# Chunk loop of a decoder layer: in each paired half the state products are issued first and the output products behind them, instead of in turn

## The chip, the cores and the metric

The kernel runs on one core of one Trainium2 chip. The metric is the device time of one execution in microseconds. The median of the runs before the change is 1487.71 us.

## The reference

One decoder layer on x of shape (4, 1024, 256): x plus a gated delta-rule attention of layernorm(x), plus a differential cross attention on a context of 64 tokens, plus a mixture-of-experts feed-forward. The change lies in the first part, a recurrence over the tokens with 16 heads of 16 x 16 state:

```python
def step(Sst, inp):
    qt, kt, vt, bt, gt = inp
    Sd = gt[..., None, None] * Sst
    kS = jnp.einsum('bhk,bhkv->bhv', kt, Sd)
    Snew = Sd + jnp.einsum('bhk,bhv->bhkv', kt, bt[..., None] * (vt - kS))
    ot = jnp.einsum('bhk,bhkv->bhv', qt, Snew)
    return (Snew, ot)
```

## The kernel before

The 1024 tokens are cut into 8 blocks of 128 tokens (times 4 batch rows), and each block into 8 chunks of 16 tokens. Within a chunk the recurrence is turned into small matrix products; from chunk to chunk the state is carried. Three stages of neighbouring blocks run side by side on every engine, in an order written out by hand in the tables `ORDERS`: a word such as `cs.3.1` is one call of the stage function `cs_` with chunk 3 and half 1, and the engines are tied by semaphore counters (`up` waits for one, `fin` raises one). TensorE works through its list in this order.

For each chunk c the chain of the recurrence is: `d1` (TensorE, L1943, old state times keys and queries) raises `d1_ps`; DVE's `m` (L1407) builds the operand `rq`; `cs` (TensorE) forms the state products (`state_product`, L1951) and, for the chunk before, the output products (`out_product`, L1957); DVE's `o` (L1425, L1428) sums up the output and waits for `co_ps`; DVE's `s` (L1414) updates the state and waits for `cs_ps`; the next `d1` waits for the state. On DVE, `o` of chunk c-1 stands ahead of `s` of chunk c. `z` (TensorE, L1926) prepares a later chunk; it goes over two row halves `a` in its outermost loop, over two groups g and four batch rows in the inner ones, with 64 x 32 weights and 128 moving columns.

The products of `cs` are fp32 with 32 x 64 weights and 64 moving columns. The state product takes rows 64k + 32*half, the output product the other strip of 32 rows, 64k + 32*(1-half); both take the 64 columns from 64a, and they write to different PSUM banks (k and 2 + k). A chunk is done in two halves; the second waits for the first through `cs_half`. In chunk 0 there is no output product, and the last chunk's output products are issued by `co` alone. Both products are called from `cs_`, L1966 to L1979.

Of the kernel before, what the change touches and what calls it, by code (L numbers as in the profile page):

```python
# [36 lines left out]
G = 2  # L37
# [292 lines left out]
def build(nc, x, out, weights, consts, cols, scratch, biases):  # L330
    ctx = ExitStack()
    with ctx:
# [1347 lines left out]
        def _(pe):  # L1680
# [73 lines left out]
            def first(i):  # L1754
                def up(name, k=1):
                    pe.wait_ge(ev[name].sem, ev[name].at(i, k))

                def fin(name, ins):
                    ins.then_inc(ev[name].sem, 1)
# [187 lines left out]
                def state_product(c, g, k, a, half):  # L1947

                    q, p_ = slice(64 * a, 64 * a + 64), slice(64 * k + 32 * half, 64 * k + 32 * half + 32)
                    dst = bank[k][q, 0:D].rearrange("p (h n v) -> p h n v", h=4, v=DH)[:, :, 2 * g + half, :]  # L1950
                    return mm(dst, zc_ring[p_, c % 4, 2 * a + g, 1, :], rq[p_, c % 2, (2 * a + g) * 64:(2 * a + g) * 64 + 64].rearrange("p (h v) -> p h v", h=4), start=True, stop=True)  # L1951

                def out_product(c, g, k, a, half):

                    q, p_ = slice(64 * a, 64 * a + 64), slice(64 * k + 32 * half, 64 * k + 32 * half + 32)
                    dst = bank[2 + k][q, 0:D].rearrange("p (h n t) -> p h n t", h=4, t=CH)[:, :, 2 * g + half, :]
                    return mm(dst, rq[p_, c % 2, (2 * a + g) * 64:(2 * a + g) * 64 + 64], zc_ring[p_, c % 4, 2 * a + g, 0, :].rearrange("p (h t) -> p h t", h=4), start=True, stop=True)  # L1957

                def cs_(c, half):

                    if half:
                        up("cs_half", c + 1)
                    else:
                        up("r", c + 1)
                        up("zc", min(c + 3, 8) if c else 1)
                        if c > 1:  # L1966
                            up("o", c - 1)
                    for g in range(G):
                        for k in range(2):
                            for a in range(2):  # L1970
                                last = state_product(c, g, k, a, half)
                                if c:
                                    last_out = out_product(c - 1, g, k, a, 1 - half)
                    if half == 0:
                        fin("cs_half", last_out if c else last)
                    else:
                        fin("cs_ps", last)
                        if c:
                            fin("co_ps", last_out)  # L1979
# [19 lines left out]
                def wo_(k):  # L1999
                    if k == 0:  # L2000
# [9 lines left out]

                return {"turn1": turn1, "rot": rot, "unrot": unrot, "cond": cond, "gate": gate, "proj": proj, "db": db, "btr": btr, "brep": brep, "sum": sum_, "vturn": vturn, "decay": decay, "grow": grow,
                        "raw": raw, "z": z, "d1": d1, "cs": cs_, "co": co, "onorm": onorm, "wo": wo_}

            def second(j):
# [258 lines left out]
```

How the kernel before makes its waits and increments, by code:

```python
    def wait(self, step=None):  # L92
        step = self.count if step is None else step
        self.eng.wait_ge(self.sem, self.i * self.per + step if self.per else step)
# [510 lines left out]
        @block.sync  # L606
# [11 lines left out]
            load_weights(["cin"], ld_cin)
            load_scratch(ramp, "ramp", ld_ramp)
            sp.dma_start(bias_row, biases[:, :]).then_inc(ld_b, 16)
            load_weights(["dw", "ctrl"], ld_proj)
            for n, name in enumerate(("wk", "wv", "ctx")):
                load_scratch(stage[:, 512 * n:512 * n + 512], name, ld_ctx)
            load_scratch(stage[:, 2048:3072], "ctxd", ld_ctx)
            load_weights(["wo", "ffu"], ld_rest)
            sp.wait_ge(su["split"], 1)
            for n in range(3):
                sp.dma_start(bias3[n:n + 1, :].rearrange("o (p n) -> o p n", p=NBR), bias_part[n]).then_inc(ld_b3, 16)
# [7 lines left out]
            def store(n):  # L639
                sp.wait_ge(ev["done"].sem, ev["done"].at(n, 2))
                sp.dma_start(rows(out, n).rearrange("b p d -> p b d"), ot[:, :, :]).then_inc(x_out.sem, 16)
# [1 line left out]
            def load_residual(i):  # L644
                sp.wait_ge(ev["tinv"].sem, ev["tinv"].at(i))
                load(xres, xres_in, i)
# [1 line left out]
            def values(i):  # L649
                sp.wait_ge(ev["vt_sb"].sem, ev["vt_sb"].at(i, 2))
                if i:
                    sp.wait_ge(v_in.sem, v_in.at(i - 1, 64))
                    sp.wait_ge(ev["r"].sem, ev["r"].at(i - 1, 8))
# [31 lines left out]
                def fin(name, ins):  # L686
                    ins.then_inc(ev[name].sem, 1)
```

## Time and profile before

| | |
|---|---|
| median of 3 runs | 1487.71 us (1486.2 to 1487.97) |
| profiled execution | 1491.12 us, span of its instructions 1489.1 us |
| PE busy, matmul | 1393.9 us, 94% |
| DVE busy | 1180.6 us, 79% |
| ACT busy | 835.1 us, 56% |
| chain that ended last | PE 76%, DVE 16%, ACT 5% |
| records of L1951 and of L1957 | 2048 each |

PE is TensorE's matmuls, PEld its weight loads, DVE VectorE, ACT ScalarE. The chain is followed back from the last instruction; at each step it goes to what released an instruction, or to the one ahead of it on its engine. A matmul's start in the trace is recorded, its end is modelled.

### The profile page before, as it was taken

To read this page: it belongs to the slowest core of one execution; us is meant where nothing else is said; L and a number is where in the kernel's file an instruction comes from. 1 tells how busy PE (TensorE), PEld (TensorE's weight loads), DVE (VectorE), ACT (ScalarE), POOL (GpSimd) and SP (SyncE) were. 2 spreads that over 40 slices of the span, in tenths; PEclk is the share of its full clock that TensorE was granted. 3 is DMA by queue.
4 is the path that set the end of the run, shared out by engine and by line. 5 is a ranking of instruction groups with operands and counts; after the bars stand their busy time and mean duration, and the time that the engine had idled before them with its cause. 6 is when DMAs were issued, how large, how long until landed. Compare 5 with 4: busy or idle time off the path is not lost.

```text
span 1489.1 us, 38165 instructions
## 1 busy us (share of the span) xinstructions
PE 1393.9 (94%) x15812; PEld 921.4 (62%) x15836; DVE 1180.6 (79%) x3196; ACT 835.1 (56%) x1599; POOL 218.3 (15%) x221
## 2 busy tenths in 40 slices
PE   5988999999999999999999999999999988898999
PEld 2555566656765566655766566655666557756765
DVE  6558888987898878987897878987897868965663
ACT  2455465646665565646666565655666555544453
POOL 1130220102300211102301122002300022000000
PEclk9999999999999999999999999999999999999999
DMA  6011010000100011000110001000100001000000
GB/s 239 0 30 30 2 30 29 3 1 16 30 30 2 2 39 27 10 2 15 30 30 2 1 20 25 31 1 9 36 15 3 2 15 30 17 2 16 1 1 15
DMA packets 20212, 31.27 MB, mean 21 GB/s; under 512 B 1480, under 2 KB 17864, under 8 KB 19784
## 3 DMA queue, kind: packets, MB, share of 16 engines
q1 hardware_dynamic: 20040, 28.82, 6.6%
q8 instruction: 126, 2.06, 0.6%
q14 instruction: 46, 0.38, 0.1%
HBM read 20.41 MB, written 8.39 MB: 19 GB/s over the span
## 4 chain that ended last, share of the span: by engine, by line
PE 76%; DVE 16%; ACT 5%; issue 2%; DMA 0%; POOL 0%; ACTq 0%; SPq 0%; DVEq 0%
PE bank L2139 14%; PE bank L1686 6%; PE bank L1816 6%; PE bank L2077 6%; PE four L1907 4%; PE bank L1711 3%; PE bank L2040 3%; PE bank L2062 3%; PE bank L1736 3%; PE four L1951 3%; PE bank L1819 3%; PE bank L1718 2%; PE four L1711 2%; PE four L1957 2%; PE four L1926 2%
## 5 line engine op out<-in xcount | busy, mean ns | idle before, releaser
L2139 PE MATMUL bank<-w_sb,cs 128*128 128x512 f32 x512 | 245.7, 597 | 1.2 <-ACT qkv L1029 0.3
L736 POOL TENSOR_TENSOR decayed<-state,pk 128x512 f32<-128x512 f32 x64 | 75.2, 1174 | 813.2 <-DVE state L1414 813.2
L1029 ACT ACTIVATE cs<-bank 128x512 f32<-128x512 f32 x112 | 66.7, 596 | 150.8 <-PE bank L1692 77.8
L2139 PEld LDWEIGHTS bank<-w_sb,cs 128*128 128x128 f32 x512 | 94.4, 190 | 90.3 <-issue 84.7
L2077 PEld LDWEIGHTS bank<-vx_sb,cs 128*128 128x128 f32 x896 | 108.9, 189 | 25.9 <-ACT cs L979 13.7
L2077 PE MATMUL bank<-vx_sb,cs 128*128 128x136 f32 x896 | 118.4, 283 | 5.4 <-ACT cs L979 3.7
L1816 PE MATMUL bank<-hT,w_sb 128*128 128x512 f32 (+1 forms) x224 | 110.6, 617 | 2.6 <-ACT rota L832 0.8
L971 ACT ACTIVATE cs<-cs 128x1024 f32<-128x1024 f32 x60 | 63.5, 1058 | 77.6 <-DVE cs L1504 77.5
L979 ACT COPY cs<-bank 128x512 f32<-128x512 f32 x114 | 66.4, 582 | 72.4 <-PE bank L2062 72.1
L1626 DVE SCALAR_TENSOR_TENSOR cs<-cs,rwt 128x256 f32<-128x256 f32 x196 | 85.6, 487 | 19.8 <-ACT cs L1029 19.8
L1273 DVE SCALAR_TENSOR_TENSOR qkv<-pre,l_sb,qkv 128x512 f32<-128x512 f32 x144 | 100.2, 746 | 0.0
L1498 DVE TENSOR_REDUCE pkc<-bank 128x8 f32<-128x512 f32 x116 | 75.1, 684 | 28.6 <-PE bank L2040 28.6
L771 ACT ACT_TABLE_LOAD x66 | 84.7, 1283 | 1.2
L2062 PE MATMUL bank<-c_sb,cs 128*128 128x128 f32 x456 | 73.3, 284 | 11.7 <-DVE cs L1525 8.2
L2040 PE MATMUL bank<-kbx,cs 32*128 32x256 f32 x464 | 77.1, 400 | 1.4 <-ACT cs L966 1.4
L1951 PE MATMUL four<-rq,shared 32*64 32x64 f32 x2048 | 61.9, 230 | 17.1 <-DVE rq L1407 9.4
L1686 PE MATMUL bank<-cs,w_sb 128*128 128x256 f32 (+1 forms) x304 | 75.2, 385 | 1.3 <-DVE cs L1561 0.9
L1951 PEld LDWEIGHTS four<-rq,shared 32*64 32x64 f32 x2048 | 44.1, 131 | 49.6 <-DVE rq L1407 22.0
L1504 DVE TENSOR_TENSOR cs<-bank,pkc 128x512 f32<-128x512 f32 x116 | 74.2, 681 | 0.0
L2062 PEld LDWEIGHTS bank<-c_sb,cs 128*128 128x128 f32 x456 | 49.1, 141 | 40.5 <-issue 27.7
L718 POOL TENSOR_TENSOR shared<-kn,c_sb 128x512 f32<-128x512 f32 x32 | 34.3, 1071 | 256.7 <-DVE kq L1310 219.5
L1414 DVE SCALAR_TENSOR_TENSOR state<-four,c_sb,decayed 128x128 f32<-128x128 f32 x256 | 71.5, 342 | 0.0
(284 smaller groups left out, 3090.7 us busy)
## 6 DMA issues: line engine op xcount, KB each, us to landing
xt<-in_x SPq DMA_DIRECT2D x8, 512.0 KB, 4.8
vscr<-qkv SPq DMA_DIRECT2D x8, 512.0 KB, 2.6
vT<-vscr SPq DMA_DIRECT2D x32, 128.0 KB, 4.4
Tm<-in_x SPq DMA_DIRECT2D x8, 512.0 KB, 3.8
out<-cs SPq DMA_DIRECT2D x8, 512.0 KB, 2.9
w_sb<-in_weights SPq DMA_DIRECT2D x1, 3656.0 KB, 18.8
w_sb<-in_weights SPq DMA_DIRECT2D x1, 1456.0 KB, 8.5
cs<-in_scratch SPq DMA_DIRECT2D x3, 256.0 KB, 8.4
```

Source lines behind the costliest of these rows:

```text
L736: fin("dec", tt(decayed[:, :, :, :], state[:, :, :, :], eGC[:, c, :].unsqueeze(1).unsqueeze(3).to_broadcast([P, 4, G * B, DH]), ALU.mult))
L771: nc.scalar.preload_act_table_set(name)
L1273: ins = stt(dst, pre[:, n % 4, :, t:TB + t], L("conv", 4 * n + t, 4 * n + t + 1), dst, ALU.mult, ALU.add)
L1498: highest[a] = link(red(mx[:, a, :], sc[a], AX.X, ALU.max))
L1626: ins = stt(comb[:, b, :], src, wgt, comb[:, b, :], ALU.mult, ALU.add)
L1686: last = mm(dst, lhs(k), rhs(k), start=k == 0, stop=k == n - 1)
L1816: mm(dst, ctrl[:, k, at:at + n], hT[:, k, :], start=k == 0, stop=False)
L1951: return mm(dst, zc_ring[p_, c % 4, 2 * a + g, 1, :], rq[p_, c % 2, (2 * a + g) * 64:(2 * a + g) * 64 + 64].rearrange("p (h v) -> p h v", ...
L2040: last = mm(scores(j, u, a)[:, 256 * f:256 * f + 256], qx[r:r + 32, f, b * TB:b * TB + TB], kbx[r:r + 32, f, b, :], start=True, stop=True)
L2062: last = nc.tensor.transpose(turned_bank(j, u, n)[:, h * P:h * P + P], prob[:, 4 * n + h, :], ident)
L2077: last = mm(values_bank(j)[:, 34 * h:34 * h + 136], probT_of(j, u)[:, h, :], vx_sb[:, at:at + 136], start=True, stop=True)
L2139: mm(dst, x1T[:, k, b * TB:b * TB + TB], ew[:, k, ep * 512:ep * 512 + 512], start=k == 0, stop=False)
```

## The change

The loop over g in `cs_` is split in two. The 8 state products of a half are issued first, then its 8 output products. The waits, the signals and what they hang on (the last state product, the last output product) stay.

```diff
@@ -1969,8 +1969,10 @@
                         for k in range(2):
                             for a in range(2):
                                 last = state_product(c, g, k, a, half)
-                                if c:
-                                    last_out = out_product(c - 1, g, k, a, 1 - half)
+                    for g in range(G if c else 0):
+                        for k in range(2):
+                            for a in range(2):
+                                last_out = out_product(c - 1, g, k, a, 1 - half)
                     if half == 0:
                         fin("cs_half", last_out if c else last)
                     else:
```

On TensorE, before the change, the first half of chunk 1 in the first block stands so (the first 8 of its 16 products; each row is one product, L1951 the state products, L1957 the output products):

```order
L1951 MATMUL four<-rq,shared 64x4x16 [waits zc,r]
L1957 MATMUL four<-shared,rq 64x4x16
L1951 MATMUL four<-rq,shared 64x4x16
L1957 MATMUL four<-shared,rq 64x4x16
L1951 MATMUL four<-rq,shared 64x4x16
L1957 MATMUL four<-shared,rq 64x4x16
L1951 MATMUL four<-rq,shared 64x4x16
L1957 MATMUL four<-shared,rq 64x4x16
```

After the change both halves of this chunk, and its neighbours on the engine, are:

```order
L1819 MATMUL bank<-rotb,w_sb 128x512 [waits cond]
L1951 MATMUL four<-rq,shared 64x4x16 [waits zc,r]
L1951 MATMUL four<-rq,shared 64x4x16 x7
L1957 MATMUL four<-shared,rq 64x4x16 x8
L1951 MATMUL four<-rq,shared 64x4x16 [waits cs_half]
L1951 MATMUL four<-rq,shared 64x4x16 x7
L1957 MATMUL four<-shared,rq 64x4x16 x8
L1736 MATMUL bank<-c_sb 128x128 x7
```

The first output product has moved from the second place of a half to the ninth; nothing has moved across a wait or past another stage. The orders of VectorE, ScalarE, GpSimd and SyncE are the same before and after.

## Rows read from the trace of the kernel before

**Rows 1.** The page: span, busy time by engine, clock in 40 slices.

```profile
span 1489.1 us, 38165 instructions
PE 1393.9 (94%) x15812; PEld 921.4 (62%) x15836; DVE 1180.6 (79%) x3196; ACT 835.1 (56%) x1599; POOL 218.3 (15%) x221
PEclk9999999999999999999999999999999999999999
```

**Rows 2.** The page: the chain that ended last, by engine.

```profile
PE 76%; DVE 16%; ACT 5%; issue 2%; DMA 0%; POOL 0%; ACTq 0%; SPq 0%; DVEq 0%
```

**Rows 3.** Groups by line and shape: busy us, mean ns | idle before.

```profile
L1957 PE MATMUL four<-shared,rq 32*64 32x64 f32 x2048 | 62.3, 230 | 1.6 <-issue 0.9
L1951 PE MATMUL four<-rq,shared 32*64 32x64 f32 x2048 | 61.9, 230 | 17.1 <-DVE rq L1407 9.4
```

**Rows 4.** Timeline of PE, two paired halves: start us, us each.

```profile
610.96 0.27 PE L1951 MATMUL four<-rq,shared 32*64 32x64 f32 x1 [0.46 <-DVE rq L1407]
610.96 0.27 PE L1957 MATMUL four<-shared,rq 32*64 32x64 f32 x1
610.97 0.27 PE L1951 MATMUL four<-rq,shared 32*64 32x64 f32 x1
...
611.01 0.27 PE L1957 MATMUL four<-shared,rq 32*64 32x64 f32 x1
611.07 0.22 PE L1951 MATMUL four<-rq,shared 32*64 32x64 f32 x1
...
611.23 0.22 PE L1957 MATMUL four<-shared,rq 32*64 32x64 f32 x1
611.59 0.27 PE L1951 MATMUL four<-rq,shared 32*64 32x64 f32 x1
...
611.86 0.22 PE L1957 MATMUL four<-shared,rq 32*64 32x64 f32 x1
612.01 0.33 PE L2062 MATMUL bank<-c_sb,cs 128*128 128x128 f32 x1
```

**Rows 5.** Chunk 0: one half in the timeline, the same in the chain.

```profile
603.07 0.46 PE L1951 MATMUL four<-rq,shared 32*64 32x64 f32 x16
603.14 0.39 PE four L1951 x16
```

**Rows 6.** Chain in order of time: a call of `z`, a 128-column group.

```profile
710.74 0.44 PE bank L1718 x4
...
764.89 0.62 PE four L1926 x32
```

**Rows 7.** Two windows at the start of a `z`, L1926 alone.

```profile
595.51:595.56 0.05, 0.04 (x4) 1.00 1.09 389
595.56:595.61 0.05, 0.05 (x8) 1.00 0.98 348
```

**Rows 8.** Chain: the first and the last paired half on it, of 100.

```profile
134.63 0.26 PE four L1951
...
1334.23 0.20 PE four L1951
```

**Rows 9.** What L1414 and L1425 waited for; who waited for L1957.

```profile
L1425 DVE TENSOR_SCALAR M<-four,c_sb x64: 319/350/352, 135.9 to 1360.4; 128x128 f32<-128x128 f32 x64
its engine sat idle before it (us, times) until:
  PE four L1957: 21.7, 26
L1414 DVE SCALAR_TENSOR_TENSOR state<-four,c_sb,decayed x256: 319/342/352, 128.3 to 1359.8; 128x128 f32<-128x128 f32 x128
its engine sat idle before it (us, times) until:
who waited for it (us, times):
...
  DVE M L1425: 21.7, 26
  PEld four L1951: 14.8, 53
```

## The prediction

> **What bounds the kernel now.** I read the page's busy shares first [rows 1]: TensorE is busy 94% of the 1489.1 us span and its granted clock stands at full speed in every slice, so neither the clock nor a second engine explains the time. The chain that ended last [rows 2] says the same: 76% of it is PE, 16% DVE, 5% ACT. In such a kernel a piece of PE time that grows is mostly paid, unless it grows in one of the few stretches where PE waits anyway. The groups of instructions [rows 3] then give the size of what is moved: 2048 records of the state products (L1951) and 2048 of the output products (L1957), each 230 ns in the mean, yet only about 62 us of busy time each, so most of each record's time lies under its neighbours.
>
> The timeline of one paired half shows how they lie [rows 4]. A half issues 8 state and 8 output products and leaves 32 matmul records, two to a product, with S (L1951) and O (L1957) taking turns. They come in four rounds of eight: eight starts from 610.96 to 611.01, then the ninth at 611.07, the last at 611.23. The records take 0.27 or 0.22 us each, so all eight of a round run at the same time. This fits the code: S and O of a pair use different 32-row strips, `a` picks one of two 64-column strips, so a group g has 4 S tiles and 4 O tiles, all different. The two records of a product and the two groups g use the same tile again, which makes the four rounds, 0.06 us apart (the first gap, with the first weight load in it, is 0.11 us).
>
> Cost of a half on PE: from the second half's first start at 611.59 to the next full-width matmul at 612.01 is 0.42 us, for 32 records [rows 4]. The first chunk has no output products, so its halves show a group of 4 tiles alone: 16 records, 0.39 us from start to the next work [rows 5]. Half as many records cost nearly the same; the tile's own four turns set the time, not the count.
>
> **The change, part by part.** Nothing is added or removed: same products, same shapes, same waits, same two signals. Only the order inside a half changes, in chunks 1 to 7 of 8 tiles: 7 x 8 x 2 = 112 halves. Chunk 0 (S alone) and `co` (O alone) issue as before.
>
> Step 1, the start of the O tiles. Before, the first O record starts 0.01 us or less behind the first S record. Now eight S products are ahead of it. How fast products enter the array is seen in [rows 4]: eight products in 610.96 to 611.01, 7 ns each, so the first O enters at 8 x 6.7 = 54 ns. The four second-group S products find their tiles occupied; the question is whether they block the O behind them. The nearest case in this trace is `z` (L1926), whose loop has `a` outermost: eight products on the 4 tiles of one row half, then eight on the 4 tiles of the other. If the second row half had to wait for the first, its first record could not come before the first half's turns are over. A turn of 128 columns takes 0.44/4 = 0.11 us in L1718 (full array, 128 columns), so 4 turns are 0.44 us and the two halves in sequence 0.88 us. The whole of `z` takes 0.62 us [rows 6]. And counted in windows, 4 records are running in the first 50 ns and 8 in the next 50 [rows 7], when no tile of the first four can be through its first turn. So the second four tiles start about 54 ns in, exactly eight entries behind, and run beside the first.
>
> Step 2, the sum for a half. O behind S by 54 ns, then four turns as in [rows 5]: 0.39 + 0.054 = 0.444 us against 0.42, that is +0.024 us. Bounds: nothing if O also slips in between S's turns without a lag (0), and 2 x 0.39 - 0.42 = +0.36 us if the O group waits for the whole S group and its drain.
>
> Step 3, how many halves are paid. Following the chain through all of the loop, records of 100 of the 112 paired halves stand on it; the first is at 134.63 us, the last at 1334.23 [rows 8]. The other 12 lie at places where DVE or ACT set the time. 100 x 0.024 = +2.4 us; all 112 would be 2.7.
>
> Step 4, the two signals. In the second half `cs_ps` hangs on the last S, which now comes up to 0.03 us earlier than before (16 records alone end their starts a little sooner than 32). The one that waits for it is the DVE state update L1414. It never sat idle for a PE result [rows 9]: DVE does `o` (L1425) of the chunk before ahead of it, and that waits for `co_ps`, 21.7 us in 26 times. `co_ps` hangs on the last O, which is now 0.024 us later. So the earlier signal gives nothing and the later one is the one waited for. These 26 waits are not added to step 3: the chain runs through PE or through them, not both. `cs_half` hangs on the last O as well; the second half's start waits on it in 53 cases, 14.8 us [rows 9], and that wait moves along, already in the 112 halves.
>
> No DMA, no other engine's queue and no PSUM buffer changes its order. What is queued behind the longer half is the next full-width matmul, which is what step 2 counts.
>
> Sum: +2.4 us. The profiled execution took 1491.12 us around its 1489.1 us span; the runs' median is 1487.71, 0.2% lower, and the difference is added to that: **1490.1 us**.
>
> One page speaks against this. The rows show that records of different tiles interleave: in [rows 4] the two records of one product are not neighbours, and S and O alternate through all four rounds. The Trainium skill, "TensorE: Matmul & The Clock Gate", Part 3, says that only weight loads are pulled ahead when their row group differs, and that matmuls start and end strictly in program order. By that rule the O group could only start behind the S group's last turn, which is the rival "in order" below. The same skill's "TensorEngine Tiling (Array Packing)", Key Properties, says that different tiles run loads and matmuls in parallel, and `z` agrees (0.62 us, not 0.88).
>
> **The rivals.**
>
> *In order* (the other side, slower): the O group starts only when S's last turn has been issued. From [rows 5], S alone spends about 0.24 us from first to last start (0.46 less the 0.22 of the last record), so a half becomes 0.39 + 0.24 = 0.63 us, +0.21; times 100 is +21 us, 1509 us. With a drain between, +0.36 each, up to 1524. It decides as soon as O's first start lies behind S's last. For it: 54 ns of lag can only hide if two products may stand before one busy tile. Against it: `z` has just that, two products for each tile, and runs in 0.62. Its products load 64 rows by 32 columns and not 32 by 64, so some doubt stays. Chance 0.08.
>
> *A queue that is one turn short*: the second-group S products hold the entry until their tile's first record is done. Then O starts one turn later, 0.06 us more: +0.08 a half, 100 x 0.08 = +8 us, about 1496. For it: the first turn with its weight load is 0.11 us in [rows 4], long enough to matter. Against: again the windows of `z`. Chance 0.12.
>
> *Nothing to see*: the alternation has a cost of its own (the round of eight needs 0.05 us of its 0.06 just to enter, and the half with 32 records is 0.03 us longer than that with 16), and the S group alone is free of it; O's later start then takes up only slack in the turns. The sum is between -0.5 and +1.5 us, 1487 to 1489. Chance 0.16, in which a quarter is a gain beyond 0.2%, if the state signal after all shortens DVE's chain (56 chunks x 0.03 = 1.7 us, and more if later waits close).
>
> **How the numbers follow.** The forecast, tiles side by side and O 54 ns behind, has 0.64. Within 0.2% (3 us) is about what a measurement of this kernel can tell from no change. My +2.4 lies close to that line; with the lag uncertain by 0.01 us a half (1 us) and the medians by as much, I give a quarter of the forecast's chance, 0.16, to slower. Slower: 0.16 + 0.12 + 0.08 = 0.36. Faster: 0.04. Same: 0.60. The range must leave out at most 0.2: "in order" (0.08) is out above, the queue rival is half in, and the low end goes just below the measurement of before: 1486.5 to 1495.
>
> **What would show it.** In the profile after, a paired half should read 8 records of L1951 and, about 0.05 us after the first, the first of L1957, while S records are still to come; from first start to the next full-width matmul 0.44 to 0.45 us. `z`, `d1` and chunk 0's halves must be unchanged. The waits of L1425 for L1957 should grow by well under 1 us. If the first L1957 starts 0.24 us behind the first L1951, the tiles do not run beside each other and the forecast is wrong by step 1; if the half is 0.44 but the time has not moved, step 3 is wrong.

## The result and the profile after

The change makes the kernel slower: 1492.24 us median of 16 runs (1487.87 to 1496.75) against 1488.24 us of before (16 runs, 1486.2 to 1493.05). The ratio is 1.0029, 95% interval 1.0018 to 1.0041, that is +4.3 us (2.7 to 6.1). The forecast was +2.4 us, 1490.1 us, in a range of 1486.5 to 1495: the time lies in the range. Of the three classes the likeliest named, "within 0.2%" (0.60), did not come; by the median ratio it is "slower" (0.36), though the interval begins at 1.0018, so that a change of just under 0.2% is not excluded.

The page after. Busy time of PE is 4.0 us and of PEld 4.0 us more than in [rows 1], the other engines stay within 0.2 us. This is not the price of the change: the profiled run after had the lower mean granted clock (0.991 against 0.993), and PE's busy time goes with it (experiment 1, at 0.995, has 1391.7 us, less than before the change).

```profile
span 1492.7 us, 38165 instructions
PE 1397.9 (94%) x15812; PEld 925.4 (62%) x15836; DVE 1180.4 (79%) x3196; ACT 834.9 (56%) x1599; POOL 218.2 (15%) x221
```

The timeline of PE over one chunk's two halves, which answers to [rows 4] (start us, us, x records that follow each other without another line between):

```profile
616.65 0.28 PE L1951 MATMUL four<-rq,shared 32*64 32x64 f32 x4
616.71 0.28 PE L1957 MATMUL four<-shared,rq 32*64 32x64 f32 x4
616.76 0.24 PE L1951 MATMUL four<-rq,shared 32*64 32x64 f32 x4
...
616.93 0.24 PE L1957 MATMUL four<-shared,rq 32*64 32x64 f32 x4
617.34 0.28 PE L1951 MATMUL four<-rq,shared 32*64 32x64 f32 x4 [0.17 <-PE four L1957]
...
617.79 1.19 PE L2079 MATMUL bank<-vx_sb,cs 128*128 128x136 f32 x8
```

The first four state tiles start at 616.65, the first four output tiles 0.06 us behind, and only then comes the state tiles' second turn at 616.76. So the tiles run side by side, as forecast. The second half goes from 617.34 to 617.79, 0.45 us against 0.42. But the step from the first half to the second is 616.65 to 617.34, 0.69 us, where [rows 4] has 0.63. In 53 of the 56 chunks the second half follows the first without other work between. Over these the median start stamps (to a nanosecond or two) give 0.452 against 0.421 us for the second half, which has other work behind it, and 0.680 against 0.630 us for the first, whose own second half follows: +0.031 and +0.050. The six halves of the other three chunks, which stand alone, take 0.443 against 0.417 us. The halves of chunk 0 are unchanged (0.547 us to the second half, 0.39 us where other work follows).

Who waited for the output products (us, times). VectorE's L1425 waited 21.7 us in 26 times in [rows 9]; now it is 24.5 in 33. The row of PE itself is new beside that of its weight loads:

```profile
who waited for it (us, times):
  DVE M L1425: 24.5, 33
  PEld four L1951: 16.0, 53
  PE four L1951: 8.7, 53
```

### The profile page after: what moved, and what is told of

It reads as the page before. It is cut to its first block, busy times and chain, and to the rows that moved or that the text cites. A ratio compares the mean times of both kernels' runs of the same rounds, so it can differ in the third digit from the quotient of the medians.

```text
span 1492.7 us, 38165 instructions
## 1 busy us (share of the span) xinstructions
PE 1397.9 (94%) x15812; PEld 925.4 (62%) x15836; DVE 1180.4 (79%) x3196; ACT 834.9 (56%) x1599; POOL 218.2 (15%) x221
## 4 chain that ended last, share of the span: by engine, by line
PE 77%; DVE 16%; ACT 5%; issue 2%; DMA 0%; POOL 0%; ACTq 0%; SPq 0%; DVEq 0%
PE bank L2141 14%; PE bank L1686 6%; PE bank L1816 6%; PE bank L2079 6%; PE four L1907 4%; PE bank L1711 3%; PE bank L2042 3%; PE bank L2064 3%; PE four L1951 3%; PE bank L1736 3%; PE bank L1819 2%; PE four L1957 2%; PE bank L1718 2%; PE four L1711 2%; PE four L1943 1%
## 5 line engine op out<-in xcount | busy, mean ns | idle before, releaser
L1951 PE MATMUL four<-rq,shared 32*64 32x64 f32 x2048 | 59.1, 230 | 18.5 <-DVE rq L1407 9.6
L1951 PEld LDWEIGHTS four<-rq,shared 32*64 32x64 f32 x2048 | 41.4, 132 | 51.0 <-DVE rq L1407 22.1
L1414 DVE SCALAR_TENSOR_TENSOR state<-four,c_sb,decayed 128x128 f32<-128x128 f32 x256 | 71.4, 341 | 0.0
```

## How the times are compared

The runs of one kernel scatter by some 10 us, and the scatter goes with the mean granted clock of the run, 0.988 to 0.997. The traces show what makes it less than 1: in before's profiled run the granted clock is 0.50 (the level of 1.2 GHz) from 176.5 to 179.0 us and 1.00 (2.4 GHz) from 180 to 190, and each profiled run has a few such stretches. PE had been busy for 2.5 of the 4 us ahead of this one. A straight line through all timed runs, with one level for each kernel on each chip, has 1.38 us for each 0.001 of clock and leaves 0.8 us of scatter. Below, each experiment has its ratio with the interval as measured, and beside it the difference to the kernel before, on the same chip, at equal granted clock (standard error 0.3 us). The experiments ran in three groups (1 to 4, 5 to 8, 9 and 10) on three chips. None leaves out any of the computation.

A value at equal clock is not always what the kernel costs: where the clock itself goes with the order of the work, that part is taken out too. In experiment 10 all ten runs have 0.993 to 0.997, and the 19 of before on that chip 0.990 to 0.995; in experiment 8 all have 0.988 to 0.990 against 0.991 to 0.997. That is too regular for chance, and what makes it was not tested. If the order of the work makes it, the measured ratio is what these two kernels cost.

For each experiment, "chunk" is the time on PE from the first start of a chunk's two halves to the next full-width matmul: 1.05 us before (0.630 + 0.421), 1.13 us in the change (0.680 + 0.452).

## Experiments

The edits stand against the changed kernel, that of experiment 8 against the kernel before. Those of 3, 4, 6, 9 and 10 are shortened to their loops and signals.

**1. State products first in the first half only.**

```diff
+                    turned = half == 1
                     for g in range(G):
                         for k in range(2):
                             for a in range(2):
                                 last = state_product(c, g, k, a, half)
+                                if c and turned:
+                                    last_out = out_product(c - 1, g, k, a, 1 - half)
-                    for g in range(G if c else 0):
+                    for g in range(G if c and not turned else 0):
```

> State products first only in the first half of each chunk; in the second half they take turns as before. Two theories. ENTRY ONLY: a half grows by the entry of the output products behind eight state products, 0.03 us, in either half alike (0.421 to 0.452 us from first start to the next full-width matmul); then 56 halves x 0.031 x 0.9 on the chain = +1.6 us. ENTRY AND SIGNAL: the semaphore that hangs on the last output product comes 0.05 us later, more than the 0.03 us by which its record starts later; the first half ends in such a wait, so it grows from 0.630 to 0.680 us to the second half's start: 56 x 0.05 x 0.9 = +2.5 us. In the profile the second halves must stay at 0.42 us. Rival CHANCE: the 0.29% of the whole change is no cost of the order, and this comes out at 0.

Measured 1.0012 (0.9999 to 1.0026), +1.5 us at equal clock. The timeline of PE (first half, then the last record of the second and what follows):

```profile
613.84 0.28 PE L1951 MATMUL four<-rq,shared 32*64 32x64 f32 x4
613.90 0.28 PE L1957 MATMUL four<-shared,rq 32*64 32x64 f32 x4
...
614.52 0.27 PE L1951 MATMUL four<-rq,shared 32*64 32x64 f32 x1 [0.17 <-PE four L1957]
...
614.80 0.22 PE L1957 MATMUL four<-shared,rq 32*64 32x64 f32 x1
614.94 0.38 PE L2082 MATMUL bank<-vx_sb,cs 128*128 128x136 f32 x1
```

The first half takes 0.68 us to the second one's start, the second 0.42. So the 0.05 us belong to the first half, whatever the second does. In time the two theories stand at +1.6 and +2.5; the result is at the smaller one, but the trace has the larger step. So only about half of the 2.9 us that 56 such steps make was paid, and why was not found. CHANCE would need five standard errors by the value at equal clock; the ratio alone does not exclude it.

**2. State products first in the second half only.** The edit is the same with the halves exchanged.

> State products first only in the second half. ENTRY ONLY: +1.6 us, as for the first half alone. ENTRY AND SIGNAL: on PE the second half is followed by other work and no wait of its own, so 0.031 us a half, 56 x 0.031 x 0.9 = +1.6 us, and a little more where VectorE waits for co_ps (26 waits x 0.05 us = at most 1.3 us, partly the same path): +1.6 to +2.3 us. Both halves' sum should come near the +4.3 us of the whole change. Rival CHANCE: 0.

Measured 0.9998 (0.9987 to 1.0009); its runs had the higher clock, 0.9938 against 0.9926 in the mean, and at equal clock it is +1.3 us. By the ratio alone this run is inconclusive. The timeline of PE, the start of the second half and what follows it:

```profile
614.93 0.28 PE L1951 MATMUL four<-rq,shared 32*64 32x64 f32 x4
...
615.38 0.38 PE L2082 MATMUL bank<-vx_sb,cs 128*128 128x136 f32 x1
```

The second half is 0.45 us, the step between the halves stays at 0.630 in the median. The two halves add up to +2.8 us, somewhat below the +3.8 of the whole (experiment 5).

**3. Blocks within a group.**

```diff
 for g in range(G):
     for k, a: last = state_product(c, g, k, a, half)
+    for k, a: last_out = out_product(c - 1, g, k, a, 1 - half)
-for g, k, a: last_out = out_product(c - 1, g, k, a, 1 - half)
```

> Blocks within a group: 4 state products, 4 output products, then the same for the second group. Eight different tiles are entered one behind the other before a tile is used again, as in the kernel before. If the cost is that of products entered ahead of the first output product on tiles that are already busy, it is gone: 0.42 us a half, 0.63 to the second half, time that of before within 0.05%. If merely the order state before output costs (switching between row strips or lines less often), part of +4.3 us stays; if alternation itself had a cost, this is faster than before by 0.01 us a half, 1 us.

Measured 0.9996 (0.9983 to 1.001), +0.2 us at equal clock. The timeline of PE, a first half and the start of the second:

```profile
614.89 0.28 PE L1951 MATMUL four<-rq,shared 32*64 32x64 f32 x4
614.92 0.28 PE L1957 MATMUL four<-shared,rq 32*64 32x64 f32 x4
615.00 0.24 PE L1951 MATMUL four<-rq,shared 32*64 32x64 f32 x4
...
615.52 0.28 PE L1951 MATMUL four<-rq,shared 32*64 32x64 f32 x4
...
615.95 1.19 PE L2078 MATMUL bank<-vx_sb,cs 128*128 128x136 f32 x8
```

0.63 and 0.43 us, as before the change. Neither "state before output" nor the blocks cost anything that is seen. What costs in the change is that products for tiles already taken stand ahead of products for free ones. The rival "nothing to see" has no support left either: by it alternation has a cost of its own, but without alternation nothing is won.

**4. Output products first.**

```diff
-for g, k, a: last = state_product(...)
 for g, k, a: last_out = out_product(...)
+for g, k, a: last = state_product(...)
-fin("cs_half", last_out if c else last)
+fin("cs_half", last)
```

> The mirror: the 8 output products of a half first, the 8 state products behind them; cs_half hangs on the last state product, the last one issued. On PE the same: 0.45 us a half, 0.68 to the second half, so +4 us by PE alone. co_ps now comes early (about 0.53 us after the half's start, as for a group of output products alone, against 0.637 before), and cs_ps late (0.687). If VectorE's wait for co_ps (26 waits) is really the one that is paid and its wait for cs_ps lies under the four output instructions of o, this gives back up to 26 x 0.1 = 2.6 us: +1.5 to +4 us. If cs_ps matters, it is as slow as the change or slower, +4.5 us or more.

Measured 1.0014 (0.9999 to 1.0028), +2.0 us at equal clock. On PE the mirror costs the same (0.68 and 0.45 us), and `co_ps` comes at 0.528 us after its half's start. VectorE's wait for it is down, from 24.5 us in the change and 21.7 before it:

```profile
L1425 DVE TENSOR_SCALAR M<-four,c_sb x64: 319/349/352, 135.3 to 1362.8; 128x128 f32<-128x128 f32 x64
its engine sat idle before it (us, times) until:
  PE four L1957: 19.0, 26
```

L1414, which waits for the later `cs_ps`, still never sits idle for it. So some of the path goes through VectorE's `o`, and not through `cs_ps`; that the 2 us less come from just this was not isolated.

**5. The change once more.**

> The changed kernel once more, beside the three others on one chip. ENTRY AND SIGNAL expects +2.8 us (the two halves' costs of the runs so far added: +1.5 and +1.4 us at equal granted clock) to +4.1 us (56 chunks x (0.031 + 0.050) us x 0.9). ENTRY ONLY expects +2.4 to +2.8 us.

Measured 1.0029 (1.0017 to 1.0041) on another chip than experiments 1 to 4, +3.8 us at equal clock. The trace has 0.452 and 0.681 us again. ENTRY AND SIGNAL had +2.8 to +4.1, ENTRY ONLY at most +2.8, three standard errors below.

**6. The signal between the halves split.**

```diff
 second half:
+    state products wait for cs_half (the first half's last state product)
+    output products wait for out_half (the first half's last output product)
-    all wait for cs_half (the first half's last output product)
```

> The changed order, with the signal between the halves split in two: the second half's state products wait for the first half's state products alone, and its output products wait for the first half's output products. Nothing is left out. If signals come in program order, that of the first eight products comes 0.53 to 0.55 us after the half's start, as in chunk 0 (0.547), and the second half starts there and not at 0.680; its output products start at 0.69 at the earliest, so the pair of halves ends its starts at 0.93 instead of 0.985 us (0.904 in the kernel before). PE is then 0.03 us a chunk above the kernel before, 56 x 0.03 x 0.9 = +1.4 us, and the wait for co_ps is 0.05 us shorter than before (1.22 against 1.27 us from the chunk's start): together about +0.5 to +1.5 us, 2 to 3 us less than the change. If instead the signal comes when the whole group has drained, the second half starts at 0.68 as in the change and nothing is won.

Measured 1.0007 (0.9996 to 1.0018), +2.1 us at equal clock, against +3.8 for the change. The timeline of PE:

```profile
613.84 0.28 PE L1951 MATMUL four<-rq,shared 32*64 32x64 f32 x4
613.89 0.28 PE L1957 MATMUL four<-shared,rq 32*64 32x64 f32 x4
...
614.39 0.34 PE L1951 MATMUL four<-rq,shared 32*64 32x64 f32 x8
614.54 0.27 PE L1957 MATMUL four<-shared,rq 32*64 32x64 f32 x1
...
614.93 1.19 PE L2083 MATMUL bank<-vx_sb,cs 128*128 128x136 f32 x8
```

The second half's state products start 0.55 us behind the first half's, exactly as in chunk 0, where no output product exists: a signal on the eighth product is not held up by the eight behind it. The output products of the second half start at 614.54, and the next full-width matmul follows at 1.09 us here, 1.099 in the median, 0.046 us above before. 56 x 0.046 x 0.9 = +2.3 us is near what was measured. My expectation of +0.5 to +1.5 missed in two places: it had 0.03 us a chunk on PE instead of 0.046, and it took VectorE's earlier `co_ps` for a gain. L1425 does wait 1.1 us less than in [rows 9] (20.6 us in 25 times), but no gain shows in the time.

**7. Output first, with the split signal.** Experiments 4 and 6 together.

> Output products first and state products behind, with the split signal: the second half's output products wait for the first half's output products, its state products for the first half's state products. On PE as in the split signal with state first: 0.93 us to the last start of the pair, +1.4 us against the kernel before. But co_ps, on which VectorE waits 26 times, hangs on the eighth product of the second half: 0.547 + 0.528 = 1.08 us after the chunk's start, against 0.630 + 0.637 = 1.27 us. If these waits are on the path, they give up to 26 x 0.19 = 5 us; the wait for cs_ps (1.22 us) lies under the four instructions of o. Expected -3 to 0 us against the kernel before. If cs_ps is what is waited for after all, +1 to +2 us.

Measured 1.0001 (0.9987 to 1.0015), +1.0 us at equal clock, against an expected -3 to 0. L1425 now waits 17.3 us in 18 times, 4.4 us less than in [rows 9], and PE takes 1.099 us for a chunk, which makes +2.3 us as in experiment 6. So if the shorter wait is what differs, some 1.3 of the 4.4 us came back. No version here is shown to beat the kernel before.

**8. Other work between the halves.**

```diff
-... -pw.0.1 cs.4.0 cs.4.1 +proj.5.0 +proj.5.1 ...
+... -pw.0.1 cs.4.0 +proj.5.0 cs.4.1 +proj.5.1 ...
```

> The kernel before (products in turn), with other work between the two halves: in 18 places of the order tables where cs.c.0 and cs.c.1 stand next to each other, the next piece of another stage is moved between them. It prices the wait that ends in cs_half: a half takes 0.42 us where other work follows and 0.63 where its own second half follows. If this is paid in full, each filled place gives 0.21 us back, some 46 of 56 chunks: -8 to -10 us. Against it the state's chain is later by the piece that was moved in (0.2 to 1.7 us); if that chain sets the time as much as PE's work does, -2 us or even slower.

Measured 1.0224 (1.0201 to 1.0247), +33 us as measured and +28 at equal clock: a clear miss of the expectation, also of its pessimistic side in size. VectorE's `o`, here L1420, tells where the time goes:

```profile
L1420 DVE TENSOR_SCALAR M<-four,c_sb x64: 341/350/352, 135.7 to 1391.7; 128x128 f32<-128x128 f32 x64
its engine sat idle before it (us, times) until:
  PE four L1952: 65.7, 48
```

65.7 us in 48 times, against 21.7 in 26, 44 us more. The reading is that the state's chain (d1, m, cs, o, s) has hardly any slack at these places: a piece put ahead of the second half delays `co_ps`, `o` and `s` behind it, and so the next chunk. Which of the 18 places cost most was not measured. The share of 76% PE on the chain [rows 2] did not say that.

**9. A smaller dose: six products ahead.**

```diff
-8 state, 8 output
+6 state, 4 output, 2 state, 4 output
```

> A smaller dose: 6 state products, 4 output products, 2 state, 4 output. Before the first output product stand two state products, not four, whose tile is still taken. ENTRY expects the first output record 40 ns behind the first state record (6 x 6.7) instead of 54, and a half of 0.43 to 0.44 us, between 0.421 (none on a taken tile) and 0.452 us (four); the wait between the halves between 0.630 and 0.680. Time +1.5 to +3 us. If the cost is of the block as such, 0.452 and 0.680, +4 us.

Measured 1.0016 (1.0002 to 1.0031), +3.0 us at equal clock. The timeline of PE:

```profile
613.36 0.28 PE L1951 MATMUL four<-rq,shared 32*64 32x64 f32 x4
613.40 0.29 PE L1957 MATMUL four<-shared,rq 32*64 32x64 f32 x4
...
614.04 0.28 PE L1951 MATMUL four<-rq,shared 32*64 32x64 f32 x4 [0.18 <-PE four L1957]
...
614.48 0.50 PE L2080 MATMUL bank<-vx_sb,cs 128*128 128x136 f32 x2
```

The first output record is 0.04 us behind, as 6 x 6.7 ns says (0.040 or 0.044 in the stamps), and a half is 0.44 us (0.438 in the median), between the two doses. With 0, 2 and 4 products for taken tiles ahead the half is 0.421, 0.438 and 0.452 us: about 8 ns for each. The signal does not go in such steps: the step between the halves is 0.681, as large as in the full change.

**10. Two products of one tile behind each other.**

```diff
-for g in range(G): for k, a: last = state_product(c, g, k, a, half)
+for k, a: for g in range(G): last = state_product(c, g, k, a, half)
 for g, k, a: last_out = out_product(c - 1, g, k, a, 1 - half)
```

> The changed order with the state products' two groups brought together: the two products of one tile follow each other (g innermost), then the next tile; the output products behind as in the change. It tests how far ahead the array takes products for a tile that is still taken. If it takes them all and lets other tiles start, tiles start 13 ns apart, the output products still at 54 ns, and a half is 0.45 us: time as the change, +4 us. If a product for a taken tile holds up what is behind it (the rival IN ORDER in a milder form), each tile's first record waits 0.06 to 0.11 us for the one before: the state products alone take 0.3 to 0.4 us longer, 112 halves x 0.3 x 0.9 = +30 us.

Measured 1.0024 (1.001 to 1.0037), that is +3.6 us, with runs of high clock (0.9957 against 0.9931); +6.9 us at equal clock. The timeline of PE:

```profile
616.54 0.30 PE L1951 MATMUL four<-rq,shared 32*64 32x64 f32 x4
616.60 0.28 PE L1957 MATMUL four<-shared,rq 32*64 32x64 f32 x4
...
617.27 0.31 PE L1951 MATMUL four<-rq,shared 32*64 32x64 f32 x4 [0.21 <-PE four L1957]
...
617.72 1.19 PE L2079 MATMUL bank<-vx_sb,cs 128*128 128x136 f32 x8
```

A product for a taken tile does not hold up the next tile: the four tiles start 13 ns apart, the output tiles at 0.06 us, a half is 0.45 us as in the change. Neither of the two cases of the expectation had what did grow, the step between the halves: 0.730 us. 56 x (0.031 + 0.100) x 0.9 = +6.6 us, against 6.9 at equal clock. In what was measured half of this is missing, because the clock was higher.

The runs beside the sum 56 chunks x (chunk on PE - 1.05 us) x 0.9, with the medians of the start stamps. Experiment 8 is left out, as its halves do not follow each other:

| | step + half, us | sum, us | at equal clock, us |
|---|---|---|---|
| before | 0.630 + 0.421 | | |
| 1 first half only | 0.681 + 0.421 | +2.6 | +1.5 |
| 2 second half only | 0.630 + 0.452 | +1.6 | +1.3 |
| 3 by group | 0.630 + 0.421 | 0 | +0.2 |
| 4 output first | 0.680 + 0.453 | +4.1 | +2.0 |
| 5 the change | 0.681 + 0.452 | +4.1 | +3.8 |
| 6 split signal | 0.548 + 0.550 | +2.3 | +2.1 |
| 7 output first, split | 0.548 + 0.550 | +2.3 | +1.0 |
| 9 six ahead | 0.681 + 0.438 | +3.4 | +3.0 |
| 10 tile twice | 0.730 + 0.452 | +6.6 | +6.9 |

The sum holds within 0.5 us in six of the nine. It is 1.1 to 2.1 us too high in experiments 1, 4 and 7. In 4 and 7 VectorE's wait for the output products is shorter than before the change; in 1 it is longer (24.1 us in 33 times), and the shortfall stays open.

## Why the prediction was right, and where it was off

**What bounds the kernel**: right for this change. Where PE grows by some hundredths of a microsecond a chunk, about eight or nine tenths are paid (table, rows 5, 6, 9 and 10). Experiment 8 adds that the state's chain is nearly as tight. The row of clock digits was read as full speed in every slice, but a 9 stands for 90% or more: the mean was 0.993, and its changes from run to run are what makes the scatter.

**Step 1, tiles side by side, the first output product 54 ns behind**: right. The first output record is 0.06 us behind the first state record and ahead of the state tiles' second turn. The analogy to `z` held. "In order" is refuted: state products' second turns start behind output products that stand later in the program, and experiment 10 shows the queue taking two products for one tile. The Trainium skill, "TensorE: Matmul & The Clock Gate", Part 3, says that matmuls start strictly in program order. This trace does not agree, and the measurement decides: all 16 state records stand ahead of the first output record in the program, and their last start is at 0.243 us, where the first output record's is at 0.054 or 0.062. The rival of a queue one turn short falls with the same rows: it would have put the first output record at 0.11 us or later.

**Step 2, +0.024 us a half**: this is the step that was mis-sized, and in two ways. The second half, with other work behind it, grew by 0.031 us: the first output record starts at 0.062 us and not at 0.054, so the 32 starts end at 0.305 us and not at 0.297, and 0.39 + 0.062 = 0.452 us is what it takes. Both lags occur: 0.054 in the six halves that stand alone, which take the 0.443 us of the forecast, and either one in the first halves. `z` in the trace of before has both too, 0.053 or 0.054 us in 50 of its 63 stretches and 0.061 or 0.062 in 12; the windows of 50 ns [rows 7] were too coarse to tell them apart. What decides between them was not found. And the half that is followed by its own second half grew by 0.050, because the signal on the last output product comes later than the start of its record explains. 0.024 for both should have been 0.031 and 0.050, +0.081 us a chunk and not +0.047. That is 56 x 0.081 x 0.9 = +4.1 us, against 4.3 measured, and 3.8 at equal clock in experiment 5. That the time still fell into the range is in part luck: the range was not drawn for the signal, whose term is the larger of the two and stands in no step of the forecast. Experiments 1 and 2 separate the two terms in the trace.

**Step 3, 100 of 112 halves paid**: in line with experiments 5, 6, 9 and 10. In experiment 1 less was paid than by this share, and where output products come first (4, 7) as well, so it is no fixed share.

**Step 4, the signals**: the sentence that the wait on `cs_half` "moves along" was wrong, it grows by the missing 0.02 us a chunk. That an earlier `cs_ps` gives nothing agrees with experiment 6. The waits of L1425 were to grow by well under 1 us; they grew by 2.8, in 33 instead of 26 times.

**The class**: with +2.4 against a line of 3 us I left 0.01 us a half for the doubt in the lag and nothing for the signal, which no row of before showed for such an order. But there was a hint: in the trace of before the second half follows 0.547 us after the first where only one kind of product is issued (`co`, and chunk 0 where its halves stand together) and 0.630 us in the others, 0.08 more, where the last start is only 0.03 later. That difference was there to be read before.

## What to carry to other kernels

Small products on separate tiles of the array should be issued so that all free tiles are fed before any tile gets its second product; whether they alternated singly or in blocks made no difference here. A product behind others for taken tiles was not blocked, but paid 7 to 8 ns for each of them, and a signal at the end of the group can pay more than that. When a group ends in a semaphore, compare the time from start to signal and not only that from start to the next matmul. And before filling a wait with other work, ask who waits for what stands behind it: the gap of 0.21 us was cheap, delaying the recurrence was not (+33 us). Last, look at the granted clock of each run before comparing differences of 0.1 to 0.3%, and at whether it goes with the kernel.

## What the runs showed of the hardware

The time from a group's first start to the start that its signal releases does not follow the last record's start. It takes 0.547 us for 8 products on 4 tiles (last start 0.243), 0.630 for 16 in turn or by group (0.270 or 0.274), 0.681 for six ahead (0.283 or 0.291) and for the full block (0.297 or 0.305), 0.730 for a tile's two products behind each other (0.297 or 0.305). Where two last starts are given both occur, and the step is the same to 2 ns. VectorE sees the same where it waits for `co_ps` (`o` starts 0.528, 0.637, 0.687 and 0.737 us after the half), so it is the signal and not PE's own wait. The last three steps are 0.05 us apart, the first is 0.08 away (0.11 for VectorE), and they depend on the order of entry; experiment 6 shows that products behind the signalling one don't matter. What makes the steps was not found.
